# GpSimd makes the two fp16 parts of the normalized output one subtraction sooner in its order

## What is computed

```python
h = jnp.maximum(_layernorm(x, axis=-1), 0.0)
q, k, v = (split_heads(h @ W.T) for W in (Wq, Wk, Wv))
a = jnp.einsum('bhnd,bhmd->bhnm', q, k) * scale + (adj + adj)[:, None]
row_nonzero = jnp.any(a != 0, axis=-1, keepdims=True)
a = jnp.where(row_nonzero, a, -jnp.inf)
p = jax.nn.softmax(a, axis=-1)
p = jnp.where(jnp.isnan(p), 0.0, p)
o = jnp.einsum('bhnm,bhmd->bhnd', p, v)
x = x + o.transpose(0, 2, 1, 3).reshape(B, N, D) @ Wo.T
```

## Time and profile before

| what | value |
|---|---|
| median of 3 runs | 1030.49 us (1030.35 to 1031.45) |
| the profiled execution | 1030.06 us, its span 1028.3 us |
| TensorE busy | 980.3 us, 95% of the span |
| ScalarE busy | 930.1 us, 90% |
| GpSimd busy | 886.2 us, 86% (588.7 of it in line 394) |
| VectorE busy | 880.8 us, 86% |
| TensorE's granted clock | 0.98 of full speed over the span |

### The profile page before, as it was taken

One profiled execution on the slowest core, in us unless ns is written; L12 is line 12 of the kernel. 1 busy time (PEld: TensorE's weight loads), 2 busy tenths in 40 slices (PEclk: granted clock), 3 DMA queues, 4 the chain that ended last, 5 costly groups with the idle time before them and its releaser, 6 DMA issues.

```text
span 1028.3 us, 34209 instructions
## 1 busy us (share of the span) xinstructions
PE 980.3 (95%) x11596; PEld 662.6 (64%) x11596; DVE 880.8 (86%) x3218; ACT 930.1 (90%) x3025; POOL 886.2 (86%) x1064
## 2 busy tenths in 40 slices
PE   6779999999999999999999999999999999999976
PEld 5556666666666666676666666666666666666733
DVE  6788998888899888899888889988888998888873
ACT  3499999999999999999999999999999999999992
POOL 1189998999999999999999999999999999999894
PEclk9899999999999999999999999999999999999978
DMA  6089999999999899999999999999999998999995
GB/s 245 11 144 173 190 185 170 191 181 187 187 188 194 174 187 175 190 186 189 188 176 185 182 186 183 192 172 189 179 186 190 187 196 173 187 175 167 164 173 128
DMA packets 569582, 182.62 MB, mean 178 GB/s; under 512 B 542784, under 2 KB 550976, under 8 KB 569408
## 3 DMA queue, kind: packets, MB, share of 16 engines
q1 hardware_dynamic: 569408, 180.43, 93.8%
HBM read 29.36 MB, written 16.78 MB: 45 GB/s over the span
## 4 chain that ended last, share of the span: by engine, by line
PE 40%; POOL 31%; ACT 19%; issue 6%; DVE 2%; DMA 1%; ACTq 0%; SPq 0%; POOLq 0%; DVEq 0%
PE ps L953 26%; POOL p L394 17%; ACT probs L488 13%; PE ps L1025 5%; PE ps L971 5%; POOL xn L374 4%; POOL o_lo L416 4%; ACT p L501 4%; POOL o_hi L413 2%; POOL rstd L368 2%; PE ps L836 2%; ACT v_hi L528 2%; POOL norm L403 2%; DVE w_max L589 1%; PE ps L999 1%
## 5 line engine op out<-in xcount | busy, mean ns | idle before, releaser
L394 POOL TENSOR_TENSOR p<-probs,p 128x512 f16<-128x512 f32 x512 | 588.7, 1160 | 86.9 <-ACT p L501 82.7
L488 ACT ACTIVATE probs<-logits,row_min 128x256 f32<-128x256 f32 x1024 | 508.7, 502 | 2.6 <-DVE row_min L669 2.6
L669 DVE CUSTOM_DVE_ANT_0 logits<-ps,adj_s,sigma 128x256 f32<-128x256 f32 x1024 | 441.3, 476 | 20.2 <-PE ps L971 13.2
L501 ACT ACTIVATE p<-probs 128x512 f16<-128x512 f32 x512 | 318.6, 622 | 0.0
L953 PE MATMUL ps<-ht_hi,w_hi 128*128 128x256 f16 x1024 | 279.7, 273 | 1.2 <-DVE q_lo L731 1.2
L953 PE MATMUL ps<-ht_hi,w_lo 128*128 128x256 f16 x1024 | 279.3, 273 | 0.0
L953 PE MATMUL ps<-ht_lo,w_hi 128*128 128x256 f16 x1024 | 279.3, 273 | 0.0
L488 ACT ACTIVATION_READ_ACCUMULATOR probs<-logits,row_min 128x1 f32 x1024 | 200.2, 196 | 0.0
L953 PEld LDWEIGHTS ps<-ht_hi,w_hi 128*128 128x128 f16 x1024 | 100.2, 98 | 21.7 <-issue 6.8
L953 PEld LDWEIGHTS ps<-ht_lo,w_hi 128*128 128x128 f16 x1024 | 100.3, 98 | 14.6
L953 PEld LDWEIGHTS ps<-ht_hi,w_lo 128*128 128x128 f16 x1024 | 100.3, 98 | 11.7
(11 more groups left out here) (84 smaller groups left out, 1659.1 us busy)
## 6 DMA issues: line engine op xcount, KB each, us to landing
xs<-in_x SPq DMA_DIRECT2D x32, 512.0 KB, 4.5
out<-xs SPq DMA_DIRECT2D x64, 256.0 KB, 2.6
adj_raw<-in_adj SPq DMA_DIRECT2D x32, 256.0 KB, 4.0
pt<-p SPq DMA_TRANSPOSE x512, 3.4
w_nat<-in_L_gnn_Wq SPq DMA_DIRECT2D x1, 1024.0 KB, 6.4
w_nat<-in_L_gnn_Wk SPq DMA_DIRECT2D x1, 1024.0 KB, 9.1
w_nat<-in_L_gnn_Wv SPq DMA_DIRECT2D x1, 1024.0 KB, 11.3
w_nat<-in_L_gnn_Wo SPq DMA_DIRECT2D x1, 1024.0 KB, 13.2
```

What stands on the lines that cost most here:

```text
L394: g.tensor_tensor(p16[:, c % 2, k, 1], probs[:, h % 4].rearrange("p u n -> p (u n)"), p16[:, c % 2, k, 0], ALU.subtract).then_inc(p_split, 1)
L488: e = a.activation(probs[:, h % 4, u, :], logits[:, h % 4, u, :], ACT.Exp, bias=row_min[:, t.par(d), u, h:h + 1], scale=-1.0, accum_out=ro ...
L501: a.activation(p16[:, c % 2, k, 0], probs[:, h % 4].rearrange("p u n -> p (u n)"), ACT.Copy)\
L669: v.tensor_tensor_reduce(out=logits[:, h % 4, u, :], in0=ps[:, S_BANK + h % HC, N * u:N * u + N], in1=adj_s[:, t.par(d), u, :], scale=sigm ...
```

## The change

In GpSimd's program the condition under which `take_o` is called moves one step ahead, for all four groups. VectorE's, TensorE's, ScalarE's and SyncE's programs are the same as before.

```diff
-                    if s in (3, 7) and t.prev:
+                    if s in (2, 6) and t.prev:
                         take_o(t, -1, NC - 2 + s // 4)
-                    if s in (11, 15) and t.cur:
+                    if s in (10, 14) and t.cur:
                         take_o(t, 0, s // 4 - 2)
                     split_probs(t, s)
```

## The result

| | before | after |
|---|---|---|
| median | 1030.49 us (5 runs, 1029.55 to 1031.45) | 1036.31 us (5 runs, 1034.52 to 1037.19) |
| profiled execution, its span | 1030.06, 1028.3 | 1034.52, 1032.7 |
| ratio | | 1.006, 95% interval 1.0047 to 1.0073 |
| VectorE busy | 880.8 us, 86% | 934.7 us, 91% |

The account below looks back on a forecast made before the run. Bound: a ring from TensorE's V through ScalarE's probabilities and GpSimd's subtractions to `o_lo` and TensorE's j=4. 1030.06 + 9.6 (29 slots x 0.33) - 1.1 = 1038.6, with 0.4 to the median 1039.0 us; range 1035 to 1043.

Parts of the forecast that it names:

- What bounds: Each slot, a ring through TensorE, ScalarE and GpSimd: TensorE's output projection (j=4) waits for `o_lo`, losing 0.52 us per slot.
- s=6: Step 6 of a slot: `o_lo` comes 1.12 us earlier, the 0.52 lost at j=4 goes; gain 0.52 per slot.
- s=10: Step 10: `some` falls into head 10's subtraction and ends sooner, so TensorE's values wait less; estimated gain 0.1 us.
- s=14: Step 14: GpSimd's later subtraction fills its 1.01 us pause, holding line 753 and `some`; VectorE 1.1 us late.
- Rival (1): VectorE isn't held, or `some` slips in ahead of p(15); 0.52 gain per slot stays, 1014.3 us; chance 0.27.
- The meeting at 983.84: Line 753's instruction took 0.48 us instead of 0.18 beside an `o_hi` from 983.89; cited as evidence of VectorE and GpSimd excluding each other.
- s=2: Step 2: GpSimd waits 1.1 us for `o_norm`, `neg_mean` is held, TensorE 1.03 late at j=2; slot 0.33 longer.
- Rival (2): `neg_mean` isn't held for long, `xn` binds `turn_h`; +0.06 us per slot, 1031.1 us, no change; chance 0.11.
- rival (3): `some` of s=11 loses the race into p(11), delaying `norm_t`; slot 0.36 us longer still, 1049.4 us; chance 0.10.
- The sum: Whole kernel: 29 slots x 0.33 = +9.6 us, last slot -1.1, from 1030.06 to 1038.6 in the profiled execution.
- its last term: Last slot: the 2.3 us wait for `o_lo` shrinks by one subtraction, -1.1 us; no layer norm runs there.

Follow-up runs that it names:

- the run with both edits: Changed kernel with line 753's test made at s=4 on two columns instead, and `neg_mean` behind the first `q_lo`: 1009.99 us, ratio 0.9809.

## Why the prediction was right

**What bounds, and s=6: right.** 0.52 at j=4, and about 0.1 through `some`. s=6 alone shortens the slot by 0.60 (0.52 + 0.10, less 0.02 more of waiting for `xn`). The owner of the 0.1 was wrong: s=10 adds nothing to s=6.

**s=14: right.** GpSimd waits 0.40 for `o_norm` (forecast 0.4), p(14) holds line 753 for 0.94 (0.9) and p(15) holds `some` for 0.85 (0.9). The run without line 753 shows that this is the cause: the next link vanished with it. Rival (1) hung on VectorE not being held. Its slot of 29.6 to 29.7 is what s=6 alone and the run with both edits have, and not the change. The rule of the Trainium skill cited in the prediction (SBUF — State Buffer, section "Who interferes with whom") agrees with the three meetings shown above. The meeting at 983.84 in the earlier trace rows, which the prediction also counts for it, fits in its end alone: there VectorE's instruction starts 0.05 ahead of GpSimd's and is the one held.

**s=2: right.** GpSimd's wait 1.09 (1.1), `neg_mean` 0.99 (1.0), TensorE late at j=2 by 1.00 from start to start in the mean (1.03), `turn_h` no longer waiting (0.08 of it before, as taken), the slot +0.31 (+0.33). Rival (2), a short `neg_mean`, is out: it takes 0.986 in the median. Not foreseen were holds of `some` at s=7 (1.02, where it took 0.32); no wait of TensorE came of them.

**s=11, rival (3): out, but not by the margin.** The prediction put `some` 0.05 ahead of p(11), and so it is, by 0.05 to 0.07 in every slot of the steady part. VectorE, then GpSimd:

```profile
499.67 0.11 DVE L687 SCALAR_TENSOR_TENSOR some<-row_min,some_qk 128x8 f32<-128x8 f32 x1
...
499.73 1.16 POOL L394 TENSOR_TENSOR p<-probs,p 128x512 f16<-128x512 f32 x1
```

What was wrong is the step from the 983.84 instruction, "came 0.05 before `o_hi` and lost": this one came as early and wasn't held. With s=14 alone it starts within 0.02 of p(11)'s start on either side and takes 0.11 or 0.12. By the prediction's own row, rival (3) with its 1049.4 should have come. That the forecast stood here was luck.

**The sum: its last term failed.** "In the last slot the 2.3 wait shrinks by one subtraction, -1.1." The wait itself shrank by 0.93, near enough; what failed is that all else behind the last `neg_mean` was put at nothing. The steady part came as said: the last `neg_mean` moved from 932.3 to 941.5, +9.2 against +9.6. But from there to the end of the span it was 96.0 before and is 91.2 now, -4.8. Of the 4.8, 1.5 lie between line 753 (983.84 and 992.3) and j=4, in which the wait for `o_lo` falls from 2.28 to 1.35, and 0.7 lie ahead of that. The rest, 2.6, lies behind the start of j=4, and most of it is TensorE's speed. The kernel before, first and sixth matmul of j=4 in the last slot:

```profile
998.65 0.58 PE L953 MATMUL ps<-w_hi,o_hi 128*128 128x512 f16 x1 [2.28 <-POOL o_lo L416]
...
1000.74 0.63 PE L953 MATMUL ps<-w_hi,o_lo 128*128 128x512 f16 x1
```

and after the change:

```profile
1005.64 0.38 PE L953 MATMUL ps<-w_hi,o_hi 128*128 128x512 f16 x1 [1.35 <-POOL o_lo L416]
...
1006.72 0.38 PE L953 MATMUL ps<-w_hi,o_lo 128*128 128x512 f16 x1
```

From the first to the sixth it is 2.09 before and 1.08 after. The last twelve matmuls of line 925 show it again, 4.42 from first to last start before and 3.04 now; the two together are 2.4 of the 2.6. The granted clock in stretches of 3 us (window: length, PE busy and count, clock, DMA share, GB/s), before:

```profile
987.00:990.00 3.00, 0.96 (x23) 1.00 1.09 259
990.00:993.00 3.00, 0.88 (x20) 0.52 1.11 189
1002.00:1005.00 3.00, 3.00 (x45) 0.71 0.34 64
```

and after:

```profile
997.00:1000.00 3.00, 0.57 (x10) 0.99 1.01 193
1000.00:1003.00 3.00, 2.71 (x48) 0.50 1.02 167
1003.00:1006.00 3.00, 0.94 (x8) 0.94 0.96 184
```

In both kernels the clock falls to the lower of its two levels behind rows in which TensorE was busy for less than a third of the time. Before, it stays there from 990.1 to 1003.7, and j=4 at 998.65 falls inside; after the change from 1000.0 to 1003.3, and j=4 at 1005.64 comes behind it. It falls once more near the end, from 1017.4 to 1024.2 before and from 1023.8 to 1027.2 after. Why the low stretches are longer in the one no run here isolates. The four moves alone don't set it: the kernel before itself took 1026.05 in one execution, with a mean granted clock of 0.993, and 1030.08 in another, with 0.983. The profiled execution is 4.1 under its sum of 1038.6: 3.7 by this term, 0.4 by the slots. Its median lies 1.8 over it, where I had allowed 0.4, and so the forecast of 1039.0 is only 2.7 off. That the median's distance took back 1.4 of the 4.1 is chance.

## What to carry to other kernels

An engine's pause can be someone else's cover. The 1.01 in which GpSimd stood still was where three of VectorE's small instructions ran undisturbed, so ask of every move which other engine's short instructions stand in the pause that it fills. Try the moves of a group one by one: here one of four made all of the gain (2% alone), one was worth nothing, and two cost 0.07 and 0.17 per slot alone and 0.91 together. And when a wait goes, look one instruction further before pricing it, since the hold moved from `neg_mean` to `some` and most of the loss stayed.

## What the hardware showed unasked

- A GpSimd tensor_scalar of 128x512 with a subtraction takes 2.076 us, the one with an addition 0.767. The slow form also read its first scalar from another tile, and no run tells the operation from the operand.
- A VectorE instruction on two elements per partition (0.17 us by itself) takes 0.99 beside a GpSimd subtraction that started just before it, and the one right behind it, reading the same tile, takes 0.155. `some`, on eight elements, which starts up to 0.07 ahead of the next GpSimd subtraction, while the last one ends, took 0.11 or 0.12 in every slot.
- In the last 45 us or so of the span TensorE's granted clock was at its lower level from 990.1 to 1003.7 and from 1017.4 to 1024.2 in one kernel, and from 1000.0 to 1003.3 and 1023.8 to 1027.2 in the other. That was worth about 2.4 us, and executions of one and the same kernel differ by as much: 1026.05 at a mean clock of 0.993, 1030.08 at 0.983. The profiled spans of kernels that differ by a few us are better compared at a mark ahead of the end, such as the last `neg_mean`.
